# A graph-network kernel on one Trainium2 core: outer products of four tiles instead of two as one PSUM group and one ScalarE copy

## The reference

```python
out = relu(n_feat @ lin0_w.T + lin0_b); h = out
eh = relu(e_feat @ en1_w.T + en1_b)                      # 200000 x 128
w_e = (eh @ en2_w.T + en2_b).reshape(-1, 32, 32)         # one 32x32 matrix per edge
for _ in range(6):
    msg = einsum('ei,eio->eo', out[src], w_e)
    agg = segment_sum(msg, dst, n_nodes) + conv_bias
    h = gru_cell(relu(agg), h, ...); out = h
```

## Time and profile before

| | us |
|---|---|
| median of 3 runs (lowest to highest) | 32453.91 (32421.82 to 32461.41) |
| the profiled execution | 32659.15 |
| its span, first to last instruction | 32657.3 |
| the six conv passes together, of the span | 18466 |

### The profile page before, as it was taken

The page is one execution under the profiler, slowest core; times in us unless marked ns, Lnnn a source line. Parts: engine busy times, 40 slices in busy tenths (PEclk is TensorE's granted clock), DMA queues, the critical chain, the costliest instruction groups (busy, mean ns, idle before and its releaser), DMA issues. The chain is left out here.

```text
span 32657.3 us, 403512 instructions
## 1 busy us (share of the span) xinstructions
PE 18488.0 (57%) x104961; PEld 12879.0 (39%) x104961; DVE 11967.1 (37%) x35567; ACT 6714.5 (21%) x20858; POOL 15518.2 (48%) x15719
## 2 busy tenths in 40 slices
PE   3334332432344447766776677667766776677654
PEld 3334221221211125544554455445444554454444
DVE  5443222222477653322333233223322332233320
ACT  0000111111111113322332233223222332232210
POOL 5884566456444434443445344534443445344520
PEclk5555555655555558777887788778877887787777
DMA  3223111121121112211221122112211221122137
GB/s 94 49 49 84 49 55 46 52 55 48 49 80 64 45 35 68 64 53 50 67 65 56 49 69 64 53 50 67 63 53 49 69 65 53 50 68 62 55 112 314
DMA packets 1256771, 2157.89 MB, mean 66 GB/s; under 512 B 744415, under 2 KB 1032120, under 8 KB 1116522
## 3 DMA queue, kind: packets, MB, share of 16 engines
q10 hardware_dynamic: 423840, 1341.95, 12.1%
q0 software_dynamic: 502784, 263.58, 5.5%
q1 hardware_dynamic: 329576, 546.81, 4.9%
HBM read 1721.40 MB, written 761.91 MB: 76 GB/s over the span
## 5 line engine op out<-in xcount | busy, mean ns | idle before, releaser
L772 POOL DMA_INDIRECT sb_xg<-node_rows,sb_src_c x14112 | 13409.7, 950 | 14872.3 <-SPq L790 8843.3
L908 PE MATMUL banks<-sb_work,sb_eh_sb 128*128 128x256 f32 x29184 | 8322.4, 439 | 2070.6 <-issue 2000.4
L908 PEld LDWEIGHTS banks<-sb_work,sb_eh_sb 128*128 128x128 f32 x29184 | 6306.8, 222 | 3839.5 <-issue 2648.6
L861 DVE TENSOR_TENSOR sb_work<-sb_xs,banks_p 128x2048 f32<-128x2048 f32 x1824 | 4172.2, 2288 | 9462.2 <-remote 6267.3
L965 ACT ACTIVATE sb_work<-banks 128x512 f32<-128x512 f32 x7296 | 4266.9, 598 | 11240.0 <-remote 6478.3
L894 PE MATMUL banks_p<-sb_work,sb_en 128*32 128x256 f32 x29184 | 3193.4, 399 | 1707.1 <-issue 1631.4
L851 DVE COPY sb_xs<-sb_xg 128x32 f32 x14592 | 1809.4, 193 | 2812.4 <-issue 2606.6
L894 PEld LDWEIGHTS banks_p<-sb_work,sb_en 128*32 128x32 f32 x29184 | 1134.9, 110 | 3472.3 <-issue 3012.7
L365 POOL DMA_INDIRECT slots<-sb_rows,sb_slot_u x1600 | 2105.9, 1316 | 783.7 <-issue 767.9
L1370 PE MATMUL banks<-sb_hot_code,sb_hot_row 128*128 128x392 bf16 x2432 | 1170.0, 506 | 1868.9 <-DVE sb_hot_code L1318 1382.9
L1155 PE MATMUL banks_s<-sb_fold,sb_s 128*128 128x32 f32 x608 | 191.8, 408 | 3261.7 <-DVE sb_s L1094 2936.1
(11 more groups left out here) (284 smaller groups left out, 14596.8 us busy)
## 6 DMA issues: line engine op xcount, KB each, us to landing
sb_eh_sb<-eh ACTq DMA_DIRECT2D x912, 1024.0 KB
adjacency<-sb_work ACTq DMA_DIRECT2D x153, 3136.0 KB
sb_work<-adjacency SPq DMA_DIRECT2D x98, 3136.0 KB, 12.5
sb_xg<-node_rows,sb_src_c POOLq DMA_INDIRECT x14112
eh<-sb_eh_sb ACTq DMA_DIRECT2D x304, 512.0 KB
sb_win_row<-window_rows SPq DMA_DIRECT2D x100, 488.3 KB
slots<-sb_zeros SPq DMA_DIRECT2D x19, 2368.0 KB
sb_rowin<-slots SPq DMA_DIRECT2D x152, 296.0 KB, 3.2
```

The costliest lines, as they stand in the source:

```text
L772: nc.gpsimd.indirect_dma_start(m.xg_ring[:, row % RING * D:(row % RING + 1) * D], None, m.node_dram, bass.IndirectOffsetOnAxis(ap=m.src_c[ ...
L861: V.tensor_tensor(m.spread[q], m.xs[h].rearrange("s (t i) -> s t i", i=D)[:, tiles, :].unsqueeze(3) .broadcast_to([P, TS, D, WN]), m.mask_ ...
L908: o = mm(m.ps_pair[u % 4][:, v, :, :], m.eh[h % 2][:, t * K:(t + 1) * K], m.spread[t // TS][:, t % TS, :, :], start=True, stop=True)
```

## The change

`U`, the number of groups in a batch, goes from 8 to 4. One group is now four tiles in two neighbouring banks, and `ps_four` has two such double banks in place of the four single ones of `ps_pair`; the number of banks is the same. The last of the four matmuls signals `g_done`, and ACT copies all four tiles with one instruction of 128 x 1024 elements. The counts that `g_sb` starts from and is waited for follow (4 becomes 2). The wait of DVE at line 860 and the place of `group`, after half the tiles, stay where they were, as they are written in terms of `U`.

```diff
-    U = TC // 2
+    U = TC // 4
...
                     pe.wait_ge(g_sb, n * U + u + 1)
-                    for v in range(2):
-                        t = 2 * u + v
-                        o = mm(m.ps_pair[u % 4][:, v, :, :], m.eh[h % 2][:, t * K:(t + 1) * K],
+                    for v in range(4):
+                        t = 4 * u + v
+                        o = mm(m.ps_four[u % 2][:, v, :, :], m.eh[h % 2][:, t * K:(t + 1) * K],
                                m.spread[t // TS][:, t % TS, :, :], start=True, stop=True)
                     o.then_inc(g_done, 1)
...
                         if h % 2 == 0:
-                            pe.wait_ge(g_sb, n * U + 4)
+                            pe.wait_ge(g_sb, n * U + 2)
                             pe.wait_ge(pj_sb, n + 2)
...
-            act.sem_inc(g_sb, 4)
+            act.sem_inc(g_sb, 2)
...
                 for u in range(U):
                     act.wait_ge(g_done, (n + L) * U + u + 1)
-                    t = (h % 2) * TC + 2 * u
-                    nc.scalar.activation(m.g[h // 2][:, :, t:t + 2, :],
-                                         m.ps_pair[u % 4].rearrange("k t i n -> k i t n"), copy).then_inc(g_sb, 1)
+                    t = (h % 2) * TC + 4 * u
+                    nc.scalar.activation(m.g[h // 2][:, :, t:t + 4, :],
+                                         m.ps_four[u % 2].rearrange("k t i n -> k i t n"), copy).then_inc(g_sb, 1)
...
-        m.ps_pair = [banks4[:, b, :].rearrange("k (t i n) -> k t i n", t=2, n=WN) for b in range(4)]
+        m.ps_four = [banks4[:, 2 * b:2 * b + 2, :].rearrange("k b (t i n) -> k (b t) i n", t=2, n=WN) for b in range(2)]
```

More of the change, by code:

```diff
@@ L923, in last_group @@
             def last_group():
-                pe.wait_ge(g_sb, BODIES * L * U + 4)
+                pe.wait_ge(g_sb, BODIES * L * U + 2)
                 pe.wait_ge(pj_sb, BODIES * L + 2)
```

## The result

| | before | after |
|---|---|---|
| median of 12 executions each, us | 32,490.19 | 32,591.34 |
| lowest to highest, us | 32,397.1 to 32,539.63 | 32,531.16 to 32,685.3 |
| ratio after / before, 95% interval | | 1.004, 1.0028 to 1.0051 |
| profiled execution, us | 32,659.15 | 32,550.47 |

The change costs 101 us, 0.4%, and the interval lies above the 0.2% that can be told from no change. The two profiled executions stand the other way round by 109 us: single executions scatter by more than the effect, so the two traces can show the mechanism but not the sum.

A forecast was written before the change was run, and what follows sets the result against it. PE's back-to-back work was taken as the bound, plus some 1,090 us a pass added beside POOL's gathers. Odd-batch delay 104 less 7 gave +97 us on 32,454: 32,551 us, range 32,200 to 32,800 for 8 times in 10.

The forecast's parts named there:

- The wide copy: ACT's copy of four tiles at line 965: 1.02 us, upper bound 1.19 if the second bank costs its own start.
- ACT's busy time: Half as many copies at line 965 take ACT from 4,356 to 3,721 us, 635 less, worth nothing in clear bodies.
- +0.43 us each time PE is waiting there, so 357 x 0.43 = 153 us: Odd batch's end: the longer last copy delays `sb_pj` and PE's fold by 0.43 us in 357 batches, 153 us.
- What of the 153 us reaches the end: Half of the shifts falling beside POOL's gathers are swallowed by pauses, so 0.68 of 153 us, 104, remains.
- The clock (C): Longer waits before PE's fold lower the passes' granted clock from 0.78 to 0.76: 334 us, 32,885; chance 0.06.
- Rival B: Fewer PE and ACT instructions gain in slow stretches beside gathers: 250 us below, 32,200; chance 0.28.
- Rival A: Nothing to be seen: the odd-batch shift is wholly swallowed or cancelled by gains in slow stretches, 32,454; chance 0.30.
- Double banks and fewer waits: PE's two double banks and four instead of eight `g_sb` waits a batch: taken as nothing; banks at most 137 us.
- 7 us of the pauses' ends: Odd batches ending out of a pause: two wide copies beat four by 0.07 us, 99 times, -7 us.
- What was to show it: Signs: `sb_pj` wait up about 150 us from 1,781, clear body 0.9 us longer, copy 1.02 us, ACT 635 us down.

The follow-up runs named there:

- experiments 1 to 3: Kernel before with ACT's wide copy alone: 1.0075; same, odd batches' last four tiles as two pairs: 1.0009; kernel before plus a spare copy ahead of `sb_pj`: 1.005.
- experiments 4 and 5: `sb_pj` copied early: ahead of the last three pair copies in the kernel before, 0.9913; ahead of the last wide copy in the changed kernel, 0.9914.
- experiment 6: Kernel before, but PE waits for free banks only at every second pair, asking for both: 24,695.94 us, 1.0001.
- experiments 11 and 12: Side by side on one chip, against the kernel before: first the change itself, 1.0057; second ACT's wide copy alone, PE's signals and waits unchanged, 1.0072.
- the sums first: Kernel before with PE's `sum_rows` put ahead of its fold in every batch: 24,483.64 us, 0.9914.

## Why the prediction was right, and where its steps weren't

**The verdict.** Forecast 32,551 us, +97 us or 0.30% above the median shown then; measured 32,591, which is 101 us, 0.4% (0.28 to 0.51), above the kernel before. The mechanism was the right one and the sign too: experiments 1 to 3 show, at the faster level, that nearly all of the loss hangs on the last copy of an odd batch. But two sizes in the sum were off, a third effect was missing, and they partly cancel: with the measured growth of the wait the same sum would have given 104 x 0.68 - 7 = 64 us. That 97 stands so near 101 is in part luck.

**The wide copy**, 1.02 us: 1.023 measured, and the second bank has no price of its own. **ACT's busy time**, -635 and worth nothing: -627, and experiments 4 and 5, alike to 2 us, show it worth nothing.

**"+0.43 us each time PE is waiting there, so 357 x 0.43 = 153 us"** is the step that was mis-sized. I took the difference of the two copies' durations and checked it on one timeline, that of a written-out body; the median over the trace would have shown that in most batches `sb_pj` follows the `eh` issue and not the copy. The measured difference is 0.29 us, and with my 357 batches that is 104 us.

**"What of the 153 us reaches the end"**, 0.68: at the level of the experiments PE loses 38.5 us in the bodies that it paces, and POOL's floor gives back 17.5 of them, so 0.55 reaches the end. That a shift is swallowed where gathers set the pace was right there. I had put it into the pauses, and of those the experiments can say nothing, as they had none; the 0.68 stays unchecked.

**The clock (C)** I gave 0.06, with rows 3 against it. As a case of its own, 32,885 us, it did not come. Its mechanism is real and was missing in the sum: at the faster level it is 24.4 of the 38.5 us that the change loses in bodies 2 to 25, more than the waiting itself. The granted clock of the passes fell to 0.77, below the 0.78 that the prediction had named as C's sign, and not to C's 0.76. At the first level I count 173 such groups behind 350 waits before and 221 behind 325 after, and the time at the lower clock in bodies 2 to 25 is 644 us a pass before and 688 after, in one execution each. So rows 3, with its two waits of 1.01 us and clock 0.97, was again a stretch that isn't the usual one. The Trainium skill, "TensorE: Matmul & The Clock Gate", section "A second HAM failure mode: psum-queue depth-cycling", says that small idle times between groups of matmuls make the clock swing; the traces agree, with 5.39 us in place of 3.70 behind a wait of 1.17.

**Rival B**, faster through the slow stretches, asked for idle time before line 965 to shrink. The "remote" part stayed, 6478.3 to 6536.9 us, with 3,648 copies fewer on ACT. No gain from the instructions that went away can be seen. **Rival A**, nothing to be seen, fell with the interval.

**Double banks and fewer waits**, taken as nothing: experiment 6 gives 1.0001. PE's part as a whole gives back some 31 us (experiments 11 and 12), which I hadn't counted. The 7 us of the pauses' ends were in the sum, and no run can tell them.

**What was to show it.** Two signs failed. The wait for `sb_pj` was to rise by 150 us from 1,781; it came out at 1751.9. Most of that total is the ends of pauses (342 waits, but 325 of usual length, median 1.46, make only 481 us of it), and those vary by more between two executions. The sign holds only where no pauses are: 510.8 to 639.6. And the clear body was to grow by 0.9 us: it grows by 0.6 (47.5 to 48.1), 2 x 0.29, with more bodies on the upper steps.

**What stays open:** what holds PE's results back while POOL gathers at one level and not at the other; how much of the 101 us at that level is wait and how much clock (350 x 0.29 would be 102 alone, so something is swallowed there too, if the clock costs anything); whether `sb_pj` early or the sums first win anything at that level; and the 0.06 us of experiment 12.

## What to carry to other kernels

Merging copies on an engine that is waited for saves nothing and delays whatever small result stands behind the last one: look at what the critical engine reads next, and put that copy ahead of the bulk (here 0.85%, where the merge cost 0.4 to 0.6%). Size such a delay by the median over all occurrences, not by one timeline, and look for instructions of the same queue, a DMA issue here, that already take up part of it; and see whether the timeline comes from the loop or from written-out bodies, as their code differs. An idle moment of TensorE may cost more than its length, in the lower clock behind it (24.4 us beside 14 of waiting here), and less than its length, where another engine's floor takes it up: price both.

## What the runs showed of the hardware

- Behind a wait of 1.17 us, eight tiles of matmuls (sixteen rows) took 5.39 us and not 3.70 in 273 of 450 cases, with the granted clock at 0.65 in that stretch and 1.00 before it; behind 1.46 us in 367 and, in a second execution, 343. With the wait filled by four matmuls nobody needs, and 0.28 us idle, in 130 of 438, and the kernel was 0.39% faster.
- In bodies 2 to 25 of a pass PE was at the lower clock for 117.2 us before and 166.1 after the change; half of the difference, 24.4 us, and 14 us of longer waits make up the 38.5 us that these bodies lost.
- A PSUM copy of 128 x 1024 over two banks took 1.023 us on ACT, against 0.597 for 128 x 512 in one: 0.83 ns a column, and nothing for the second bank.
- ACT's issue of a load took 0.34 us between two copies, and the next copy began 0.47 us after the issue did; with the issue 0.14 us earlier the copy began 0.13 us earlier.
- The same kernel took 32,490 us in the first comparison and 24,692 to 24,708 in the groups of the experiments. At the faster level PE was busy for 200.00 of 200 us at a clock of 1.00 while POOL issued 161 gathers, so the gathers alone don't hold PE back. The Trainium skill's rule that PE never waits on anyone ("SBUF — State Buffer", "Who interferes with whom") agrees with those runs; whether the pauses of rows 8 and 9 go against it, as the prediction has it, is open: no run shows what causes them.
